# The next chunk's score product inside the sums, and both score scans ahead of the membership compare, in a four-layer graph kernel

## The reference

```python
h   = (x @ W).reshape(n, HEADS, C)
a_s = jnp.einsum('nhc,hc->nh', h, att_src)
a_d = jnp.einsum('nhc,hc->nh', h, att_dst)
e = leaky_relu(a_s[src] + a_d[dst], 0.2)
m = segment_max(e, dst)
p = exp(e - m[dst])
z = segment_sum(p, dst)
out = segment_sum(h[src] * (p / z[dst])[:, :, None], dst)
```

## Time and profile before

| | us |
|---|---|
| median of the timed runs (9949.32 to 9965.64) | 9952.7 |
| the profiled execution, its own time | 9986.09 |
| its span | 9984.4 |
| PE busy | 7617.1 (76%) |
| POOL busy | 6220.2 (62%) |
| DVE busy | 4982.3 (50%) |
| ACT busy | 2153.3 (22%) |
| granted TensorE clock, mean | 0.816 |

### The profile page before, as it was taken

One profiled execution on the slowest core, in us unless ns is written; L12 is line 12 of the kernel. 1 busy time (PEld: TensorE's weight loads), 2 busy tenths in 40 slices (PEclk: granted clock), 3 DMA queues, 4 the chain that ended last, 5 costly groups with the idle time before them and its releaser, 6 DMA issues.

```text
span 9984.4 us, 147624 instructions
## 1 busy us (share of the span) xinstructions
PE 7617.1 (76%) x44592; PEld 6370.8 (64%) x44593; DVE 4982.3 (50%) x12729; ACT 2153.3 (22%) x7282; POOL 6220.2 (62%) x6545
## 2 busy tenths in 40 slices
PE   7999999986677777777655777777775777777774
PEld 5777777764466666666544666666664666666664
DVE  3333333331156666666422666666662566666664
ACT  1222222221122222222111222222221222222222
POOL 4777777650067777777401777777770677777772
PEclk8999898885578888888755888888886788888887
DMA  3333332220022222222100222222220222222221
GB/s 95 80 79 78 76 76 74 73 57 6 7 61 66 66 66 65 66 66 66 40 7 13 69 69 69 69 69 69 69 69 17 64 69 69 69 69 70 69 69 28
DMA packets 408173, 606.93 MB, mean 61 GB/s; under 512 B 209519, under 2 KB 288338, under 8 KB 408014
## 3 DMA queue, kind: packets, MB, share of 16 engines
q0 software_dynamic: 206336, 462.61, 19.1%
q1 hardware_dynamic: 201806, 143.95, 5.7%
HBM read 584.63 MB, written 20.80 MB: 61 GB/s over the span
## 4 chain that ended last, share of the span: by engine, by line
PE 39%; POOL 21%; issue 19%; DVE 15%; DVEq 4%; ACT 1%; DMA 1%; SPq 1%; POOLq 0%; ACTq 0%
POOL G L469 20%; PE ps L566 11%; PE ps L588 6%; PE ps L583 6%; PE ps L613 5%; DVE msg L1110 4%; DVEq L990 3%; DVE acc L1017 2%; PE ps L556 2%; PE ps L668 1%; PE ps L634 1%; DVE acc L1007 1%; DVE shared L1064 1%; DVE shared L1072 1%; PE ps L721 1%
## 5 line engine op out<-in xcount | busy, mean ns | idle before, releaser
L469 POOL DMA_INDIRECT G<-rows,idx x6448 | 6137.7, 952 | 2241.1 <-issue 1902.8
L566 PE MATMUL ps<-msg,memb 128*128 128x136 f32 (+2 forms) x12896 | 1812.0, 303 | 104.4 <-DVE msg L1110 104.1
L937 DVE TENSOR_TENSOR memb<-rel,ps 128x1664 f32<-128x1664 f32 x496 | 936.2, 1888 | 1885.8 <-PE ps L566 1885.6
L566 PEld LDWEIGHTS ps<-msg,memb 128*128 128x128 f32 x12896 | 1734.3, 210 | 134.9 <-issue 70.6
L613 PE MATMUL ps<-membT,shared 128*104 128x128 f32 x9672 | 1616.4, 334 | 2.2 <-ACT membT L760 2.2
L556 PE MATMUL ps<-ident,memb 128*128 128x128 f32 x6448 | 1117.3, 317 | 485.3 <-DVE memb L937 441.3
L613 PEld LDWEIGHTS ps<-membT,shared 128*104 128x104 f32 x9672 | 1465.1, 218 | 29.2 <-issue 3.3
L556 PEld LDWEIGHTS ps<-ident,memb 128*128 128x128 f32 x6448 | 813.3, 159 | 703.9 <-issue 386.7
L1017 DVE TENSOR_TENSOR acc<-acc,ps 128x136 f32 (+2 forms) x3472 | 1023.5, 295 | 433.8 <-DVE acc L1017 352.6
L760 ACT ACTIVATE membT<-ps 128x512 f32<-128x512 f32 x1984 | 953.0, 504 | 76.6 <-PE ps L556 65.3
L475 POOL TENSOR_TENSOR rstd<-varn,minus_half 128x4 f32<-128x4 f32 x78 | 78.6, 1008 | 1420.7 <-DVE varn L1153 1420.7
(11 more groups left out here) (205 smaller groups left out, 6048.7 us busy)
## 6 DMA issues: line engine op xcount, KB each, us to landing
G<-rows,idx POOLq DMA_INDIRECT x6448
shared<-marks_all SPq DMA_DIRECT2D x372, 156.0 KB
shared<-in_edge_attr SPq DMA_DIRECT2D x124, 256.0 KB
shared<-in_edge_attr SPq DMA_DIRECT2D x124, 160.0 KB
rows<-msg SPq DMA_DIRECT2D x39, 288.0 KB, 2.4
idx<-in_src SPq DMA_DIRECT2D x496, 6.5 KB
shared<-joins_all SPq DMA_DIRECT2D x372, 1.7 KB
rows<-msg SPq DMA_DIRECT2D x13, 256.0 KB, 2.9
```

The source lines that it names most:

```text
L469: nc.gpsimd.indirect_dma_start(G[:, b, t, 0:rows[l].shape[1]], None, rows[l], bass.IndirectOffsetOnAxis(idx[:, b, t:t + 1], 0)).then_inc(g ...
L566: last = mm(ps_sum[k // 2][:, 0:width], memb[:, b, 64 + k * P:64 + (k + 1) * P], msg[:, b, k, 0:width], start=k % 2 == 0, stop=k % 2 == 1 ...
L937: tt(memb[:, b, 64:64 + K * P].rearrange("p (k n) -> p k n", k=K), r, w, ALU.is_equal).then_inc(memb_ready, 1)
```

## The change

The change is made in layers 1 to 3; layer 0 keeps its order.

- On TensorE the score product of the next chunk (L620, now in `source_scores`) moves from the head of that chunk's `attention` to the middle of the present chunk's sums: tiles 0 to 9, then the product, then tiles 10 to 12. For chunk 0 it stands ahead of the loop.
- On TensorE the turns move: batches 0 and 1 from ahead of the tile ends (L625) to behind them; batches 2 and 3 from ahead of the carries (L634) to behind them, before the first eight tiles of target scores.
- On VectorE the membership compare moves from the head of `attention` to behind the second scan. `window_numbers` and `keep_factor` keep their place between the scans.

```diff
+    PARTED = 10
...
-            def sums(l, c, b, width, parts):
-                if c is not None:
+            def sums(l, c, b, width, k0, k1):
+                if k0 == 0:
                     pe.wait_ge(added[GR - 1], past(l, c - 1))
-                for k in range(K):
+                for k in range(k0, k1):
...
-                last.then_inc(summed, 1)
+                if k1 == K:
+                    last.then_inc(summed, 1)
...
-                sums(0, c, b, P + 1, None)
+                sums(0, c, b, P + 1, 0, K)
...
-            def attention(l, c, b, ahead=True):
+            def source_scores(l, c, b):
                 pe.wait_ge(sc_kept, gpast(l, c))
                 mm(ps_sc[b][0:JH, :], sflat[:, :], ident[:, :], start=False, stop=True).then_inc(sc_ready, 1)
-                if ahead:
-                    turn(l, c + 1, 1 - b, (0, 1))
+
+            def attention(l, c, b, ahead=True):
                 pe.wait_ge(seg_all, gpast(l, c))
...
                 last.then_inc(ends_out, 1)
                 if ahead:
-                    turn(l, c + 1, 1 - b, (2, 3))
+                    turn(l, c + 1, 1 - b, (0, 1))
                 pe.wait_ge(run_kept, gpast(l, c))
...
                 last.then_inc(carry_out, 1)
                 if ahead:
+                    turn(l, c + 1, 1 - b, (2, 3))
                     pe.wait_ge(sc_copied, gpast(l, c))
                     target_scores(l, c + 1, 1 - b, 0, 8)
...
-                sums(l, c, b, SW if l == 1 else MW, None)
+
+                width = SW if l == 1 else MW
+                sums(l, c, b, width, 0, PARTED)
+                if ahead:
+                    source_scores(l, c + 1, 1 - b)
+                sums(l, c, b, width, PARTED, K)
...
                     target_scores(l, 0, 0, 0, K)
+                    source_scores(l, 0, 0)
...
             def attention(l, c, b, h, prev=True, ahead=True):
-                if ahead:
-                    make_membership(l, c + 1, 1 - b)
                 brk, nf, nl = (marks[0:JH, b, m * P:(m + 1) * P] for m in range(3))
...
                 scan(body, marks[0:JH, b, 1:P][:, ::-1], body, segm[0:JH, P - 1:P], ALU.add, ALU.max).then_inc(seg_all, 1)
+                if ahead:
+                    make_membership(l, c + 1, 1 - b)
                 if prev:
```

## The result

The changed kernel takes 10,379.5 us (median of 4 runs, 10,339.1 to 10,398.1). The kernel before, run beside it, takes 9,959.2 us (9,949.3 to 10,003.9). The ratio is 1.0407 with a 95% interval of 1.0363 to 1.0452: 420 us slower. The forecast was 10,325 us, a ratio of 1.037. In the table further down, one run of e1 (10,422.6 us) fell in a slower state of the chip and counts neither in its median nor in its ratio.

What follows compares the result with a forecast made beforehand. GpSimd's gathers bound layers 2 and 3, the VectorE and TensorE loop layer 1. Losses of 172 and 197 us, together 369, on 9986.1 made 10,355; 33 lower for the timed median gave 10,325 us, range 10,110 to 10,540.

Steps and rivals of the forecast that it cites:

- Part 1: VectorE, first scan to rescale: the register load loses membership's cover, rescale 0.3 us later (0 to 0.5).
- rival B: VectorE's register load runs while the scan waits, rescale 0.7 us earlier than now; time 10,010 us; chance 0.09.
- Part 2: TensorE's score product inside the sums: sums end about 0.25 us later, adding nothing beyond Part 1.
- the sum: Layer 1: 123 chunks x 1.4 = 172 us; layers 2 and 3: 246 x 0.8 = 197 us; together 369 us.
- Part 3: Turns one place later on TensorE: it reaches the weights later, by 1.2 us at lower clock, 0.8 at full.
- Rival A: TensorE's sums too run slow in most chunks, layer 1 at 20.2 us a chunk; about 10,560 us; chance 0.11.
- Rival C: TensorE holds full clock behind the carries; layer 1 at 8.69 + 7.8 = 16.5 us a chunk; 9,880 us; chance 0.06.

Runs made afterwards that it cites:

- e1: The changed kernel with VectorE's register load of the window numbers moved to the head of the chunk: 10,330 us, ratio 1.0328 to the kernel before.
- e4: The changed kernel with membership back at the head of VectorE's attention, so the TensorE part alone: 10,357 us, ratio 1.0390 to the kernel before.
- e5: The kernel before with both scans ahead of membership on VectorE, nothing else: 10,705 us, ratio 1.0748.
- e6: The kernel before with the score product inside the sums, turns and VectorE order unchanged: 9,977 us, ratio 1.0019.
- e7: The kernel before with the turns moved one place later, nothing else: 10,199 us, ratio 1.0244.
- the mends: Two edits to the changed kernel, alone (e1, e2) and together (e3): 10,330, 10,169 and 9,931 us.
- e8: The changed kernel with eight more TensorE products a chunk in idle stretches, output read by nothing: 9,889 us, ratio 0.9929 to the kernel before.
- e3: The changed kernel with the register load at the head of the chunk and all turns ahead of the carries: 9,931 us, ratio 0.9976 to the kernel before.
- e2: The changed kernel with all four turn batches between the tile ends and the carries: 10,169 us, ratio 1.0208 to the kernel before.
- the filled kernels: Kernels with eight more TensorE products a chunk that nothing reads, e8, e9 and e10 among them: ratios 0.9929 to 0.9951 to the kernel before.
- e10: e8 with the register load moved to the head of the chunk: 9,896 us, ratio 0.9936 to the kernel before.
- e9: The kernel before with eight more TensorE products a chunk, read by nothing, ahead of first turns and carries: 9,928 us, ratio 0.9951.

## Why the prediction was right, step by step

- **Direction, size and place: right.** 10,379.5 us against 10,325 (range 10,110 to 10,540). By stages: +1.9 us a chunk in layer 1 where +1.4 was forecast, +0.70 in layers 2 and 3 where it was +0.8.
- **Part 1, the register load: the mechanism is shown, both its size and its price at the end were off.** The load starts only with the scan (1.38 us "issue" before L1005). So rival B fell. By the rule of the Trainium skill's page "Perfetto Trace Analysis", section Sequencer Loop, the load would have run while the scan waited; the trace does not agree, for all 97 chunks of the third view pay for it. Whether the scan waited in VectorE's queue or was held back ahead of it, the profile does not show. The size: the forecast took 1.04 us for the load from the one chunk in the earlier trace rows, but its median is 1.62 us after the change (and was before it, where membership hid it). The second scan so starts 1.90 us behind the first (3501.69 to 3503.59) and not 1.35. Message to rescale takes 9.26 us in the chunk shown against 8.39: 0.87 us later, where 0.3 (at most 0.5) was forecast. The price: e4, which hides the load again, is only 0.2 us a chunk faster in layer 1 and nothing in layers 2 and 3, where 0.3 was forecast for every chunk. In e5 the order on VectorE costs far more, but there the scans also start only behind the sums.
- **Part 2, the product: right** (e6: 19 us slower than before, no term in the sum).
- **Part 3, the turns: the right place, with a price that was under-sized in layer 1.** Rescale to message was forecast at 7.8 or 9.8 us; the chunk shown has 9.76. The forecast said half to all chunks would be slow, and took a value between; in fact the message waits in every chunk of layer 1 (85 waits). In layers 2 and 3 too the message waits in every chunk, and each costs 0.70 us; the forecast had a mixture there of chunks that lose 1.1 us and chunks that lose nothing. e7 gives the turns alone 242 us.
- **The sum as such was the weak step.** It priced each part by itself and added. The parts alone cost 7.5%, 0.2% and 2.4%, the whole 4.1%; the mends gain 0.8% and 2.0% alone and 4.3% together. That the total fell within 55 us is partly luck: layer 1 lost 62 us more than forecast and layers 2 and 3 lost 25 us less, and a later rescale that hardly reached the end stood beside slow chunks that were more frequent than assumed.
- **Rival A (the clock falls further)** was half right: the clock did fall, from 0.85 to 0.76 and 0.80, but in turns and scores and not in the sums, which ran faster than before (0.151 against 0.165 us a pass in layer 1). In e1 it is what happened in layer 1: slow sums and slow scores, 20.45 us a chunk against the 20.2 that rival A worked out.
- **Rival C (the turns fit at full clock)** did not happen by itself, but e8 brings it about: rival C had 16.5 us for layer 1 and nothing lost in layers 2 and 3, thus 9,880 us; held near the full clock the changed kernel runs at 16.56 and 16.27, 9,889 us. The total agrees by luck of its terms: it was 8.69 + 7.8, and the chunk of e8 shown above has 9.24 + 7.34.

What is shown: with TensorE's idle stretches filled and the changed order kept, the whole loss disappears, and the turns and score passes are what runs faster. What is not shown is why the changed order lowers the clock. That the idle time of TensorE ahead of the scores grew (2.95 us in the earlier trace rows, with the 1.96 us before the first turns shown under e5 and the 0.99 before the carries, to 4.12) is not enough: e1 has less of it than the changed kernel at the lowest clock, and e5 has the longest single stretch (4.29 us) at about the clock of the changed kernel. The reason that the prediction gave against rival C, that the idle time before the carries causes the drop, fits its own rows as little: 1.70 us of it stand before the score passes of 2.00 us in the earlier trace rows and 0.99 before those of 3.74 us in the earlier trace rows. The order in which turns and scores follow matters as well, and how is open. The line of the chunk of the earlier trace rows:

```profile
3515.80 0.49 PE L634 MATMUL ps<-ones,shared 1*104 1x1 f32 x4 [1.70 <-DVE shared L1072]
```

## What to carry to other kernels

Where TensorE is busy three quarters of the time and its clock changes level inside each loop pass, as here, the price of a reordering isn't the sum of the durations that it moves: read the granted clock beside every stage. Before giving up an order, try it with TensorE's idle stretches filled with products that nobody reads; here that turned 4% slower into 0.7% faster. Then give the old order the same: here it gained 0.5%, and e3, with no such products, 0.2%, so the gain over the old order is small. And a register load in an instruction stream has a place of its own. Here it hid behind a long instruction of the same engine, or ahead of an instruction that waits (e1), and it came into the open right behind a waiting one. Its duration is better taken from all its instances than from one.

## What the runs showed of the hardware

**Less chain, more time.** e1 removed a wait of over a microsecond from VectorE and layer 1 went from 18.96 to 20.45 us a chunk, at a lower clock (0.76 to 0.67): its sums took 0.211 us a pass in the mean, against 0.151, and its score passes 0.233 against 0.186.

**Equal paces with different orders.** Layers 2 and 3 run at 17.05, 17.05 and 17.07 us a chunk in the changed kernel, e2 and e4, whose orders differ by five turns and by the load, and layer 1 of the kernel before and e6 at 17.06 and 17.05. In the kernel before, layer 1 reaches that pace with fast and slow score passes in turn; in e6 the granted clock is lower (0.80 against 0.85) at the same pace. e5, e7 and the filled kernels do not show it, and no run tells why the others do.

**The same gathers differ in duration from kernel to kernel.** These are the gathers of layer 2, 5750 to 7350 us, in the kernel before, e8 and e10; the mean of one, in ns, stands before the second bar.

```profile
L469 POOL DMA_INDIRECT G<-rows,idx x1271 | 1213.7, 955 | 387.3 <-issue 384.3 <-DVE msg L1110 3.0
```

```profile
L470 POOL DMA_INDIRECT G<-rows,idx x1277 | 1210.0, 948 | 390.7 <-issue 389.8 <-DVE msg L1124 0.9
```

```profile
L470 POOL DMA_INDIRECT G<-rows,idx x1261 | 1215.8, 964 | 384.3 <-issue 382.5 <-DVE msg L1125 1.5 <-DMA idx<-in_src 0.3
```

GpSimd hardly waits for messages in all three (at most 3.0 us), yet 13 gathers take 0.21 us more in e10 than in e8 (16 ns each). That is the loss of layers 2 and 3 in e10. It is not the chip: e3, with the load early on the chip of e8, has 965 ns, and e9, with the load hidden on the chip of e10, 954. Nor is it the load's place alone: the changed kernel, with the same VectorE instructions in the same order as e8, has 968. What beside them lengthens them was not tried.
